# Normalising spread over two steps, and output transposes and output projection moved to later steps and another PSUM bank

## The reference

```python
q = rope(layernorm(x) @ Wq); k, v = split(ctx @ Wkv); k = rope(k)
w = softmax(q k^T / sqrt(8))          # per batch and head, 128 x 128
x = x + (w v) @ Wout + bout
x = x + ffn(layernorm(x))             # 32 routed experts, 6 per token, and shared ones
```

## Time and profile before

| | |
|---|---|
| median of 3 runs | 394.51 us (393.67 to 396.32) |
| the profiled execution | 392.62 us, its span 390.8 us |
| PE, DVE, ACT, POOL busy, share of the span | 83%, 62%, 52%, 38% |
| periods 1 to 12 (all parts present) | 47.85 to 185.71 us of the span |
| batches' last steps | 185.71 to 219.69 us |
| expert layer | 219.69 to 390.8 us |

### The profile page before, as it was taken

One profiled execution on the slowest core, in us unless ns is written; L12 is line 12 of the kernel. 1 busy time (PEld: TensorE's weight loads), 2 busy tenths in 40 slices (PEclk: granted clock), 3 DMA queues, 4 the chain that ended last, 5 costly groups with the idle time before them and its releaser, 6 DMA issues. The chain is left out here.

```text
span 390.8 us, 9518 instructions
## 1 busy us (share of the span) xinstructions
PE 325.1 (83%) x3094; PEld 217.2 (56%) x3094; DVE 241.2 (62%) x667; ACT 202.1 (52%) x390; POOL 146.9 (38%) x239
## 2 busy tenths in 40 slices
PE   0768999999999999999977387978998986999930
PEld 0436676767777776777655233454765753444420
DVE  4395778677677777778665445899741168444410
ACT  3236776767867777876766473643223432233310
POOL 4544443324444333444000400264588300444460
PEclk9986999999999999999999669999999899999985
DMA  7411104435444453533200033011133554933345
GB/s 180 150 34 36 30 20 136 113 107 145 120 120 125 111 141 109 142 106 93 61 22 2 14 133 129 1 29 54 55 92 91 164 166 142 304 60 38 47 47 215
DMA packets 33293, 37.93 MB, mean 97 GB/s; under 512 B 7808, under 2 KB 27568, under 8 KB 33200
## 3 DMA queue, kind: packets, MB, share of 16 engines
q1 hardware_dynamic: 22610, 22.03, 19.2%
q10 hardware_dynamic: 8030, 11.93, 10.5%
q0 software_dynamic: 2624, 3.61, 5.7%
HBM read 26.36 MB, written 8.96 MB: 90 GB/s over the span
## 5 line engine op out<-in xcount | busy, mean ns | idle before, releaser
L386 ACT ACTIVATE pw<-bank 128x512 f32<-128x512 f32 x128 | 76.7, 600 | 45.7 <-PE bank L617 34.8
L493 DVE TENSOR_REDUCE mx<-bank 128x4 f16<-128x512 f32 x128 | 87.2, 684 | 16.4 <-PE bank L593 15.8
L263 POOL TENSOR_TENSOR rot<-t 128x256 f32<-128x256 f32 x30 | 21.2, 726 | 93.1 <-DVE t L486 93.1
L606 PE MATMUL bank<-qst,kz 128*128 128x128 f16 x512 | 50.0, 221 | 4.1 <-DMA qst<-mxs 3.5
L593 PE MATMUL bank<-kz,qst 128*128 128x512 f16 x128 | 49.4, 387 | 1.8 <-issue 1.3
L606 PEld LDWEIGHTS bank<-qst,kz 128*128 128x128 f16 x512 | 37.4, 99 | 17.2 <-DMA qst<-mxs 6.3
L927 POOL DMA_INDIRECT acc<-ac,dst x16 | 23.6, 1472 | 43.4 <-ACT ac L1005 33.4
L617 PE MATMUL bank<-pw,V 128*32 128x128 f32 x1024 | 34.7, 276 | 0.0
L1253 PE MATMUL mbank<-hT,WSG 128*128 128x512 f16 (+1 forms) x144 | 32.0, 379 | 0.0
L617 PEld LDWEIGHTS bank<-pw,V 128*32 128x32 f32 x1024 | 25.9, 109 | 9.0 <-issue 6.8
L500 DVE COPY mxs<-bank 8x128 f16<-8x128 f16 x64 | 13.2, 207 | 23.6 <-PE bank L597 23.5
(11 more groups left out here) (195 smaller groups left out, 620.9 us busy)
## 6 DMA issues: line engine op xcount, KB each, us to landing
ring_gu<-in_L_ffn_w_gate_up ACTq DMA_DIRECT2D x20, 352.0 KB
kz<-kT SPq DMA_DIRECT2D x64, 64.0 KB, 2.0
ring_dn<-in_L_ffn_w_down ACTq DMA_DIRECT2D x10, 352.0 KB
ring_gu<-in_L_ffn_w_gate_up SPq DMA_DIRECT2D x8, 352.0 KB
X<-in_x SPq DMA_DIRECT2D x4, 512.0 KB, 7.3
table<-ac SPq DMA_DIRECT2D x8, 256.0 KB, 2.1
acc<-X SPq DMA_DIRECT2D x4, 512.0 KB, 3.1
out<-acc SPq DMA_DIRECT2D x4, 512.0 KB, 5.6
```

The costliest lines, as they stand in the source:

```text
L263: eng.tensor_tensor(rot[:, part], t1[:, part], t2[:, part], ALU.add).then_inc(rot_ok[w], 1)
L386: act.activation(pw[g % 4][:, :], STB[g % 2][:, :], ACT.Exp, scale=SCALE).then_inc(exp_ok, 1)
L493: dve.tensor_reduce(mx[u // 2 % 2][:, u % 2:8:2], SB[u % 2][:, :].rearrange("p (j t) -> p j t", j=4), axis=AX.X, op=ALU.max, negate=True). ...
L606: ins = pe.matmul(STB[g % 2][:, j * P:j * P + P], kz[m.par][:, j, g, :], qst[m.par][:, g, :], start=True, stop=True)
```

## The change

The output of batch b-1 is finished later and in its own bank. `normalise` is cut in two: the reciprocal comes in step 5, the product in step 6, both behind that step's `row_max`. `transpose_attn` moves from step 4 to step 7, between `transpose_max` and `logits_q`, and writes `OB` in place of `M0`. ACT's copy to `attnT` moves from step 5 to step 7, behind that step's exponential. `project_out` moves from step 6 to step 1 of the following period, and writes `OB`. The addition to X and `bn_stats` move from step 7 to step 2 of the following period, the two directly behind each other (new functions `add_out` and `statistics2`). `weigh_values(b, 0)` now waits for the addition of batch b-2, with which it shares a bank, and `project_v` no longer waits for an addition. On DVE `evac_max` and `row_max` now come ahead of `rope_cos` in step 3. There is one more period at the end, b = 17, with only the last output.

```diff
-            for n in range(12, NB + 1):
+            for n in range(12, NB + 2):
...
-                    if g == 5 and inside(o):
+                    if g == 7 and inside(o):
                         act.wait_ge(attnT_mm, o.n + 1)
                         at_least(act, wo_mm, o.n)
-                        act.copy(attnT[:, :, :], M0[:, D:2 * D].rearrange("p (c t) -> p c t", c=DK)).then_inc(attnT_ok, 1)
+                        act.copy(attnT[:, :, :], OB[o.par][:, D:2 * D].rearrange("p (c t) -> p c t", c=DK)).then_inc(attnT_ok, 1)
...
+            def normalise(m, part):
                 ob = OB[m.par][:, :].rearrange("p (x f s) -> p x f s", f=2, s=HALF)
+                if part == 0:
+                    at_least(dve, ob_mm, m.n + 1)
+                    at_least(dve, attn_ok, m.n)
+                    dve.reciprocal(rec[:, :, :], ob[:, :, :, HD]).then_inc(rec_ok, 1)
+                else:
+                    at_least(dve, attnT_mm, m.n)
+                    dve.wait_ge(rec_ok, m.n + 1)
+                    dve.tensor_tensor(attn[:, :].rearrange("p (f x d) -> p x f d", f=2, d=HD), ob[:, :, :, 0:HD],
+                                      rec[:, :, :].unsqueeze(3).broadcast_to([P, NH // 2, 2, HD]), ALU.mult).then_inc(attn_ok, 1)
+
+            def add_out(m):
+                dve.wait_ge(wo_mm, m.n + 1)
+                dve.wait_ge(x_biased, m.n + 1)
+                dve.tensor_tensor(X[:, m.n, :], OB[m.par][:, 0:D], X[:, m.n, :], ALU.add).then_inc(x1_ok, 1)
+
+            def statistics2(m):
+                dve.wait_ge(x1_ok, m.n + 1)
+                dve.wait_ge(rope_tab, 3)
+                dve.bn_stats(st2[:, m.n, :], X[:, m.n, :]).then_inc(st2_ok, 1)
...
-                    if g == 3 and inside(m3):
-                        rope_cos(m3)
                     if g % 2 == 1:
                         who, half = (b, (g + 3) // 2) if g < 5 else (m1, (g - 5) // 2)
                         if inside(who):
...
                         row_max(who, u)
+                    if g == 2 and inside(o2):
+                        add_out(o2)
+                        statistics2(o2)
+                    if g == 3 and inside(m3):
+                        rope_cos(m3)
                     if g == 4 and inside(m3):
                         rope_sin(m3)
+                    if g in (5, 6) and inside(o):
+                        normalise(o, g - 5)
...
             def project_v(m):
-                at_least(pe, x1_ok, m.n - 2)
+                at_least(pe, qst_ok, m.n)
...
-                    at_least(pe, attn_ok, m.n - 1)
+                    at_least(pe, x1_ok, m.n - 1)
...
+                    if g == 7 and inside(o):
+                        transpose_attn(o)
                     who, u = (b, g + 5) if g < 3 else (m1, g - 3)
                     if inside(who):
                         logits_q(who, u)
...
+                    if g == 1 and inside(o2):
+                        project_out(o2)
...
-                    if g == 4 and inside(o):
-                        transpose_attn(o)
...
-                    if g == 6 and inside(o):
-                        project_out(o)
```

More of the change, by code:

```diff
@@ L500, in evac_max @@
                 dve.tensor_copy(mxs[half % 2][:, :], SB[1][0:8, 0:P // 2].bitcast(F16)).then_inc(mxs_ok, 1)
-            def normalise(m):
-                at_least(dve, ob_mm, m.n + 1)
+            def normalise(m, part):
                 ob = OB[m.par][:, :].rearrange("p (x f s) -> p x f s", f=2, s=HALF)
[L505 to L510, removed]
+                if part == 0:
[15 more added lines that the diff above has]
+                dve.bn_stats(st2[:, m.n, :], X[:, m.n, :]).then_inc(st2_ok, 1)
             def period(b):
-                m1, m3, o = b + 1, b + 3, b + -1
+                m1, m3, o, o2 = b + 1, b + 3, b + -1, b + -2
                 for g in range(QUADS):
[L515 to L518, removed]
-                    if g == 3 and inside(m3):
-                        rope_cos(m3)
                     if g % 2 == 1:
@@ L629, in transpose_attn @@
                 pe.wait_ge(attn_ok, m.n + 1)
-                pe.wait_ge(qst_ok, min(m.n + 3, NB) if isinstance(m.n, int) else m.n + 3)
                 for c in range(DK):
-                    ins = pe.transpose(M0[:, D + c * P:D + c * P + P], attn[:, c * P:c * P + P], identf[:, :])
+                    ins = pe.transpose(OB[m.par][:, D + c * P:D + c * P + P], attn[:, c * P:c * P + P], identf[:, :])
                 ins.then_inc(attnT_mm, 1)
@@ L637, in project_out @@
                 for c in range(DK):
-                    ins = pe.matmul(M0[:, 0:D], attnT[:, c, :], WO[:, c, :], start=(c == 0), stop=(c == DK - 1))
+                    ins = pe.matmul(OB[m.par][:, 0:D], attnT[:, c, :], WO[:, c, :], start=(c == 0), stop=(c == DK - 1))
                 ins.then_inc(wo_mm, 1)
@@ L643, in period @@
             def period(b):
-                m1, m2, m3, o = b + 1, b + 2, b + 3, b + -1
+                m1, m2, m3, o, o2 = b + 1, b + 2, b + 3, b + -1, b + -2
                 for g in range(QUADS):
```

## The result

The changed kernel takes 399.68 us (median of 4, 399.57 to 401.25), the kernel before 394.09 us in the runs beside it. The ratio is 1.0188, interval 1.0101 to 1.0275: slower, though the interval leaves open whether by more than 2%. That is 5.6 us between the medians and 7.4 by the ratio, which leaves out the one slow execution of the kernel before (396.32 us). The forecast was 401.7, 7.2 us slower. The profiled execution took 401.25 us, 8.6 more than that of before.

The account below looks back on a forecast made before the run. PE bounds the kernel, losing time to row maxima, rope_sin and DMA. 10.67 + 0.05 + 0.38 + 0.74 + 0.27 = 12.11 us a period against 11.49; with loop and end +7.2, so 401.7 us; 397 to 405 for 8 in 10.

Parts of the forecast that it names:

- Steps 6 and 7: PE: without project_out behind logits_q of step 6, transpose_max of step 7 waits 0.74 us for DVE's row maximum.
- The product: Step 7: transpose_attn, queued ahead of logits_q, waits for DVE's product of normalise, holding up all of PE by 0.27 us.
- DVE's burst: DVE in steps 2 to 4, now with addition and statistics: PE waits 0.05 us before logits_q of step 5, 0.38 at transpose_k.
- the loop's counting: Addition to a semaphore wait on DVE in steps 2 and 3: nothing to 0.15 us a period, taken as 0.05, 0.5 in all.
- The rule of the Trainium skill: DVE: a semaphore between two vector instructions costs nothing extra; statistics 0.34 behind the addition, not 0.46, up to 1.4 us less.
- The DMA waits that go: PE's logits_k waits for maxima in step 0 (0.30 us) and step 4 (0.48 by label, period before) both vanish.
- Sum: Period 12.11 us against 11.49; twelve give +7.5 us, loop +0.5, end -0.8: together +7.2, forecast 401.7 us.
- my 10.67 us of work: PE's work in a period, 11.48 less waits of 0.14, 0.37 and 0.30; unchanged by the change.
- the end: End of the attention: the wait for attnT and the projection leave the last weigh_values; gain 0 to 1.6 us, taken as 0.8.
- Rival (a): No change: waits for rope_sin and the product vanish because DVE keeps up; period 11.46, time 393.3 us; chance 0.13.
- (b): Faster: wait at transpose_max in step 7 is covered, lost DMA waits count; period 11.10, time 389.0 us; chance 0.08.
- (c): Slower still: the DMA waits stay beside the new ones, 6.5 us more, 408.2 us; chance 0.07.

Follow-up runs that it names:

- e3: Changed kernel with V's projection moved from step 0 to step 6 of the period before, for batch b+2: 395.46 us, ratio 1.0044.
- e7: Changed kernel with project_out back in step 6, for batch b-2 in M0, addition and statistics in step 7 and at its end: 389.45 us, ratio 0.9905.
- e2: Changed kernel with transpose_attn of step 7 behind that step's logits_q instead of ahead of it: 398.4 us, ratio 1.0098.
- e4: Changed kernel with both parts of normalise back in step 3 of DVE, behind rope_cos: 405.94 us, ratio 1.028.
- e11: Kernel before, with the first of the three weight transfers that ACT issues each period in step 2 instead of step 1: 391.73 us, ratio 0.9975.
- e1: Kernel before, with only its output path moved to the bank OB, in the steps of before: 394.52 us, ratio 0.9986.
- e10: Changed kernel with only rope_cos moved back ahead of evac_max and row_max in step 3: 402.47 us, ratio 1.0251.
- e9: e7 plus transpose_attn behind logits_q of step 7 and rope_cos ahead of evac_max in step 3: 382.05 us, ratio 0.9738 to the kernel before.
- e6: Changed kernel with e2's and e3's edits, addition and statistics in step 1, and project_out ahead of the k projection: 394.24 us, ratio 1.0032.

## Why the prediction was right

**Steps 6 and 7 (0.74 us, measured 0.73).** Right in mechanism and size. Period 0 of the kernel before had shown it. e3 took 0.43 us of it away with 0.43 of cover and no other edit; in e7, with the projection back, it is gone.

**The product (0.27, measured 0.27).** Right in size (0.33 less 0.06). e2 shows that 0.17 of it can be had, since `logits_k` of step 0 then waits.

**DVE's burst (0.05 and 0.38, measured 0.20 and 0.36 to 0.45).** The mechanism held (e4), the first term was too small. The statistics started 0.56 us behind the addition inside the loop (147.77 to 148.33), not 0.46 as at the end of the attention; I had named this unknown and given it 0.05 us a period, it was 0.10 on DVE. That the loop's counting causes it is not shown. The other 0.07 came from PE, which was ready that much earlier than I had it (see the sum). The rule of the Trainium skill that was weighed there ("VectorE: DVE Perf Modes", section "The DRAIN you can't avoid") is not borne out by either row: they show 0.56 and 0.46 us where a start without a dependency comes after 0.34. Its measurement is of copies, whose dependencies it does not name; here the second instruction reads what the first writes.

**The DMA waits that go (both to nothing; measured: step 4 gone, step 0 0.26 in every second period of the loop).** The maxima of step 5 took 3.04 us from `evac_max` (151.26) to `logits_k` (154.30), not 2.69. This term was mis-sized by 0.13 us a period. That the wait of step 4 went by cover was not tested by itself: in the changed kernel the weights are also issued 0.49 us behind the maxima (133.30 and 132.82), and e11 shows that issuing them apart, there by 0.95 us, ends the wait with no more cover.

**Sum.** On top of my 10.67 us of work these waits would give 12.4 us a period, where I had 12.16 with the loop's share; measured were 12.30. The 10.67 was too large: period 9 of the changed kernel takes 12.43 us, of which 1.85 are waits, which leaves 10.58. Rows 2 held small waits that I took for work, as `transpose_max` 0.25 behind `logits_k` in step 5 and 0.22 in step 7. Periods 1 to 12 lost 9.35 us for my 8.0; the end gained 1.7 us (34.31 from 185.71 to 220.02, against 32.60 from 195.16 to 227.76) for my 0.8. Most of the two errors cancel, by luck: 7.7 us in the attention of the profiled executions, 7.2 forecast. Luck stands in the last step too. I added 1.89 us because the profiled execution of before lay below its median; the one of the changed kernel, forecast at 399.8, took 401.25 and lay 1.57 above its median. So the median came out 2.0 us below the forecast, and the profiled execution 1.4 above it.

Rival (a) asked for the waits for `rope_sin` and for the product to vanish; both stayed. (b) asked for a PE that doesn't idle in step 7; it idled in each period. (c) asked for DMA waits of 0.54 us a period to stay; 0.13 stayed.

**What the change did, part by part.** The bank: nothing (e1). Spreading `normalise`: a gain of 0.48 us a period with the wait for the product already paid (e4). Moving `project_out` out of step 6, and the addition with it into step 2: a loss of 1.00 us a period (e7 undoes these together). 0.73 of it is the idle time of step 7, by the rows; how the rest divides is not shown. `rope_cos` behind `evac_max`: nothing in the changed kernel (e10), 0.30 us lost where DVE has a gap (e9).

## What to carry to other kernels

Before moving work off a step, ask what it covers: taking 0.87 us of projection out from between `logits_q` and the `transpose_max` that waits for its row maxima left PE idle for 0.73 us, and 0.43 us of other work put there won 0.44 (e3), though PE was busy for 131.82 of 137.86 us in the kernel before. A period without the moved piece, at the start of a pipeline, shows the stall ahead of the change. Waits of one period stand for one another, so price a new one against what the others do then, and add up only what separate runs have shown to add up.

## What the runs showed that I had not expected

A small transfer was late when one of 352 KB was issued 0.02 to 0.12 us ahead of it. In the kernel before, SP issues the maxima of step 1 (L311) and ACT the weights (L121); in period 8 they stand so:

```profile
128.69 0.39 ACTq L121 DMA_DIRECT2D ring_gu<-in_L_ffn_w_gate_up  x1
128.71 0.59 SPq L311 DMA_DIRECT2D qst<-mxs  x1
```

`logits_k` of step 4 started 3.01 us behind that issue (131.72) and had waited for it. It did not wait in the periods in which the large transfer came 0.25 us behind the small one. In e11, where it comes 0.95 us behind (126.72 and 127.67), `logits_k` starts 2.34 us behind the issue (129.06) without a wait for the DMA. Moving the large transfer cut the waits from 9.9 to 2.0 us. Removing that wait gave nothing, which I had priced at 3 us.

e7 had its maxima in time in step 4 too, without a projection in step 1. There the large transfer stands 0.43 us behind the small one:

```profile
129.45 0.59 SPq L311 DMA_DIRECT2D qst<-mxs  x1
129.88 0.39 ACTq L121 DMA_DIRECT2D ring_gu<-in_L_ffn_w_gate_up  x1
```

`logits_k` starts 2.79 us behind the issue (132.24) without a wait, sooner than the 3.01 of the kernel before. So the distance of the two issues fits this as well; no run tested it in e7.

`logits_q` waited 0.7 to 1.9 us for `kz` in one of periods 1 to 3 in the profiled executions of e1, e3, e4, e6, e7 and e11 (1.94 us in period 2 of e1), and not there in the changed kernel, which is why kernels are compared here by the mean period too. What makes these transfers late was not tried and stays open.
